# Gate and up projections in column blocks of 512, 512 and 384, with five shared PSUM banks and new orders on all engines

## What is computed

```python
v = x @ W_write.T                      # chunked decay recurrence over the sequence
reads = sum over earlier tokens j of decay**(t-1-j) * (x_t . x_j) * v_j
x = layernorm(2 * x + alpha * (reads @ W_read.T))
gate = fp4(x) @ fp4(w_gate).T          # w_gate, w_up: 704 x 256
up   = fp4(x) @ fp4(w_up).T
h    = silu(gate) * up                 # 704 columns
x = layernorm(x + fp4(h) @ fp4(w_down).T)
```

## Time and profile before

| | before |
|---|---|
| median of 3 runs | 328.34 us (328.29 to 328.41) |
| the profiled execution | 328.27 us, its span in the trace 326.5 us |
| PE busy | 317.1 us, 97% of the span, 2271 matmuls |
| weight loads (PEld) busy | 304.1 us, 93% |
| DVE busy | 291.2 us, 89% |
| POOL busy | 241.2 us, 74% |
| ACT busy | 211.8 us, 65% |
| TensorE clock granted | 0.996 of 2.4 GHz, mean |

### The profile page before, as it was taken

The page is one execution under the profiler, slowest core; times in us unless marked ns, Lnnn a source line. Parts: engine busy times, 40 slices in busy tenths (PEclk is TensorE's granted clock), DMA queues, the critical chain, the costliest instruction groups (busy, mean ns, idle before and its releaser), DMA issues.

```text
span 326.5 us, 6927 instructions
## 1 busy us (share of the span) xinstructions
PE 317.1 (97%) x2271; PEld 304.1 (93%) x2271; DVE 291.2 (89%) x754; ACT 211.8 (65%) x516; POOL 241.2 (74%) x257
## 2 busy tenths in 40 slices
PE   8899999999999999999999999999999999999993
PEld 3599999998999999999999999999999999999983
DVE  3999989989988889978898888998999999999972
ACT  3678975875485658466593658747684657665773
POOL 1589968977897777767797676967597767668772
PEclk9999999999999999999999999999999999999998
DMA  5804120030013000210003010002000001000011
GB/s 194 328 2 129 46 86 2 1 131 0 0 23 141 3 32 2 98 64 18 18 19 112 32 35 1 18 16 82 1 18 32 3 0 35 33 6 28 19 49 64
DMA packets 8243, 15.71 MB, mean 48 GB/s; under 512 B 1168, under 2 KB 5264, under 8 KB 8208
## 3 DMA queue, kind: packets, MB, share of 16 engines
q1 hardware_dynamic: 7920, 15.27, 13.7%
q10 hardware_dynamic: 288, 0.00, 0.0%
HBM read 11.08 MB, written 4.19 MB: 47 GB/s over the span
## 4 chain that ended last, share of the span: by engine, by line
PE 69%; DVE 14%; ACT 6%; issue 5%; POOL 3%; DMA 2%; ACTq 0%; DVEq 0%; POOLq 0%
PE gu L1683 9%; PE gu L1687 9%; PE gu L1684 9%; PE bank L1683 6%; PE bank L1684 6%; PE bank L1687 6%; PE bank L1693 5%; PE bank L1697 5%; PE bank L1696 5%; PE bank L1771 5%; DVE h_g L1068 2%; DVE h_y L1063 2%; DVE w_raw L1174 2%; DVE hqT_lo L1202 2%; DMA scal<-in_log_alpha_dram 2%
## 5 line engine op out<-in xcount | busy, mean ns | idle before, releaser
L1683 PE MATMUL gu<-guT_hi,xqT_hi 128*128 128x352 f32 x256 | 85.3, 334 | 0.2
L1684 PE MATMUL gu<-guT_lo,xqT_hi 128*128 128x352 f32 x256 | 82.2, 322 | 0.0
L406 POOL TENSOR_TENSOR h_q<-h_g,h_ns 128x704 f32<-128x704 f32 x32 | 49.2, 1537 | 38.9 <-DVE h_g L1068 36.7
L1687 PE MATMUL gu<-guT_hi,xqT_lo 128*128 128x352 f32 x256 | 61.7, 322 | 0.0
L399 POOL TENSOR_TENSOR h_n<-w_raw,h_rs 128x704 f32<-128x704 f32 x32 | 45.5, 1426 | 5.9 <-DVE h_rs L1058 5.6
L1683 PEld LDWEIGHTS gu<-guT_hi,xqT_hi 128*128 128x128 f32 x256 | 48.1, 188 | 0.9 <-DVE w_raw L1174 0.7
L1684 PEld LDWEIGHTS gu<-guT_lo,xqT_hi 128*128 128x128 f32 x256 | 48.2, 188 | 0.1
L1687 PEld LDWEIGHTS gu<-guT_hi,xqT_lo 128*128 128x128 f32 x256 | 44.5, 188 | 0.0
L694 ACT CAST hqT_hi<-bank 128x512 fp32r<-128x512 f32 x64 | 29.8, 475 | 15.2 <-PE bank L1771 13.6
L1684 PE MATMUL bank<-dnT_lo,hqT_hi 128*128 128x256 f32 x160 | 39.1, 279 | 0.0
L1683 PE MATMUL bank<-dnT_hi,hqT_hi 128*128 128x256 f32 x160 | 39.1, 279 | 0.0
(11 more groups left out here) (127 smaller groups left out, 888.3 us busy)
## 6 DMA issues: line engine op xcount, KB each, us to landing
x_full<-in_xt_rows_dram SPq DMA_DIRECT2D x8, 512.0 KB, 3.3
xs<-in_x_rows_dram SPq DMA_DIRECT2D x8, 512.0 KB, 3.4
out_dram<-wq_gu SPq DMA_DIRECT2D x32, 128.0 KB, 1.7
w_raw<-in_w_ffn_dram SPq DMA_DIRECT2D x6, 352.0 KB, 7.7
w_pair<-in_w_attn_dram SPq DMA_DIRECT2D x1, 512.0 KB, 7.2
scal<-in_decay_dram ACTq DMA_DIRECT2D x1, 0.5 KB, 3.1
scal<-in_log_alpha_dram ACTq DMA_DIRECT2D x1, 0.5 KB, 4.9
```

The lines of the kernel that those rows point to most:

```text
L406: nc.gpsimd.tensor_tensor(blocks(h_q[:, p, 0:I]), blocks(h_g[:, p, :]), per_block(h_ns[:, p, :], HB), ALU.mult).then_inc(h_quant, 1)
L1683: nc.tensor.matmul(dst, lh, rh, start=(first and i == 0), stop=False)
L1684: nc.tensor.matmul(dst, lh, rl, start=False, stop=False)
L1687: last = nc.tensor.matmul(dst, ll, rh, start=False, stop=(end and i == len(terms) - 1))
```

## The change

`LEFT` is 704 - 512 = 192. Gate and up of a tile now take three blocks: gate columns 0 to 511 in `gu[0]`, up columns 0 to 511 in `gu[1]` (both in the call with `half` 0), and in the call with `half` 1 the last 192 gate and 192 up columns side by side in `gu[2]`, as one block of 384. For this the host packs the weight rows in the order gate[:512], up[:512], gate[512:], up[512:]. A tile takes 12 matmuls of 512 and 6 of 384 columns. `gate_silu` and `hidden` work on 512 columns for half 0 and 192 for half 1. What they compute is the same.

The bank `gu[3]` is no longer needed by gate and up and joins the shared banks: `combine`, one of the `reads`, one of the `xq_transpose`, one `h_transpose` part and one `down` move to it, and others swap banks. The semaphores that the PE calls wait for follow these tables.

The lists of PE, ACT, DVE and POOL are put into a new order throughout; the number of steps on each is the same. On SP `store(0, 0)` moves ahead of `load_x_transposed(5)`, and `load_x(4)`, `load_x(5)` and `load_x(6)` each one step earlier. The diff, cut to its core (indentation shortened):

```diff
@@ constants and banks @@
+LEFT = I - 512
-v_bank, xq_bank = (bank[2], bank[1]), (bank[0], bank[2])
-s_bank, r_bank = (bank[1], bank[3], bank[0], bank[3]), (bank[2], bank[3])
-h_bank = ((bank[1], bank[0]), (bank[1], bank[0]), (bank[0], bank[2]), (bank[0], bank[2]))
-d_bank = (bank[3], bank[1], bank[3], bank[2])
-w_bank = (bank[0], gu[:, 3, :], bank[0], gu[:, 2, :], gu[:, 1, :], gu[:, 0, :], bank[0], bank[2], bank[2])
+v_bank, xq_bank = (bank[2], bank[1]), (gu[:, 3, :], bank[2])
+s_bank, r_bank = (bank[0], bank[3], bank[0], bank[3]), (gu[:, 3, :], bank[3])
+h_bank = ((bank[1], bank[0]), (bank[1], gu[:, 3, :]), (bank[0], bank[2]), (bank[0], bank[2]))
+d_bank = (bank[3], bank[1], bank[3], gu[:, 3, :])
+w_bank = (bank[1], gu[:, 3, :], bank[0], gu[:, 2, :], gu[:, 1, :], gu[:, 0, :], bank[2], bank[1], bank[2])
+part = (slice(0, 512), slice(512, I))
+gate_of, up_of = (gu[:, 0, :], gu[:, 2, 0:LEFT]), (gu[:, 1, :], gu[:, 2, LEFT:2 * LEFT])
@@ SP queue @@
     load_x(3)
+    store(0, 0)
     load_x_transposed(5)
-    store(0, 0)
+    load_x(4)
     store(1, 1)
-    load_x(4)
     store(2, 2)
     store(3, 3)
     store(4, 0)
     load_x_transposed(6)
+    load_x(5)
     store(5, 1)
-    load_x(5)
     store(6, 2)
     store(7, 3)
     store(8, 0)
     load_x_transposed(7)
+    load_x(6)
     store(9, 1)
-    load_x(6)
     store(10, 2)
@@ gate_silu (ACT) @@
-        nc.scalar.activation(silu[:, p, half * HALF:(half + 1) * HALF], gu[:, 2 * half, 0:HALF],
-                             ACT.Silu).then_inc(silu_ready, 1)
+        nc.scalar.activation(silu[:, p, part[half]], gate_of[half], ACT.Silu).then_inc(silu_ready, 1)
@@ hidden (DVE) @@
-        c = slice(half * HALF, (half + 1) * HALF)
+        c = part[half]
-        nc.vector.tensor_tensor(h[:, p, c], silu[:, p, c], gu[:, 2 * half + 1, 0:HALF],
-                                ALU.mult).then_inc(h_ready, 1)
+        nc.vector.tensor_tensor(h[:, p, c], silu[:, p, c], up_of[half], ALU.mult).then_inc(h_ready, 1)
@@ scale_comb (DVE) @@
-        nc.vector.tensor_scalar(comb[:], bank[3][:, 0:DK * D], scal[:, 3:4], None,
+        nc.vector.tensor_scalar(comb[:], gu[:, 3, :][:, 0:DK * D], scal[:, 3:4], None,
@@ first steps of DVE @@
     w_magic_add(0)
+    w_to_grid(0)
     x_rest(0, 0)
     x_rest(0, 1)
-    w_to_grid(0)
@@ gate_up (PE) @@
-        for m in range(2):
-            w = slice(m * I + half * HALF, m * I + (half + 1) * HALF)
-            last = split_matmuls(gu[:, 2 * half + m, 0:HALF],
+        for m in range(2 - half):
+            w = slice(1024, 2 * I) if half else slice(512 * m, 512 * m + 512)
+            last = split_matmuls(gu[:, 2, 0:2 * LEFT] if half else gu[:, m, :],
@@ first steps of PE @@
     combine([])
     scores(0, 0, [])
-    scores(0, 1, [(comb_ready, 1)])
-    scores(0, 2, [])
-    scores(0, 3, [(pr_ready, 2)])
+    scores(0, 1, [])
+    scores(0, 2, [(pr_ready, 1)])
     pe.wait_ge(comb_lo_ready, 1)
     values(0, 0, [])
-    values(0, 1, [(pr_ready, 1)])
-    reads(0, 0, [(v_lo_ready, 1)])
-    w_transpose(0, [(pr_ready, 3)])
+    scores(0, 3, [(pr_ready, 2)])
+    values(0, 1, [])
+    reads(0, 0, [(comb_ready, 1)])
     reads(0, 1, [(pr_ready, 4)])
+    w_transpose(0, [(v_lo_ready, 2)])
+    w_transpose(1, [(z_ready, 1)])
+    scores(1, 0, [(pr_ready, 3)])
     w_subtract(0)
-    scores(1, 0, [(v_lo_ready, 2)])
     scores(1, 1, [(z_ready, 2)])
...
@@ loop body of PE @@
-        gate_up(k - 1, b - 1, 3, 0)
+        h_transpose(k - 5, 3, 1, [(hT_lo_ready, 2 * k - 10)])
+        gate_up(k - 1, b - 1, 3, 1)
+        scores(n + 1, 0, [(hT_lo_ready, 8 * n - 17)])
+        gate_up(k, b, 0, 0)
         reads(n, 1, [(o_ready, 4 * n - 9)])
-        xq_transpose(n - 1, 0, [(hT_lo_ready, 8 * n - 17)])
-        gate_up(k - 1, b - 1, 3, 1)
-        h_transpose(k - 4, 0, 0, [(pr_ready, k + 9)])
+        values(n + 1, 0, [(hT_lo_ready, 8 * n - 16)])
+        h_transpose(k - 4, 0, 0, [(v_lo_ready, 2 * n + 2)])
+        down(k - 5, 3, [(xqT_lo_ready, 2 * n - 1)])
+        h_transpose(k - 4, 0, 1, [(pr_ready, k + 9)])
         scores(n + 1, 1, [(z_ready, 2 * n + 2)])
-        down(k - 5, 3, [(hT_lo_ready, 2 * k - 8)])
-        gate_up(k, b, 0, 0)
-        h_transpose(k - 4, 0, 1, [(xqT_lo_ready, 2 * n - 1)])
         gate_up(k, b, 0, 1)
         h_transpose(k - 3, 1, 0, [(hT_lo_ready, 2 * k - 7)])
-        values(n + 1, 0, [(o_ready, 4 * n - 8)])
-        gate_up(k + 1, b, 1, 0)
         scores(n + 1, 2, [(hT_lo_ready, 8 * n - 14)])
         down(k - 4, 0, [(pr_ready, k + 10)])
-        h_transpose(k - 3, 1, 1, [(pr_ready, k + 11)])
+        xq_transpose(n - 1, 1, [(v_lo_ready, 2 * n + 3)])
+        h_transpose(k - 3, 1, 1, [(o_ready, k - 4)])
+        gate_up(k + 1, b, 1, 0)
+        h_transpose(k - 2, 2, 0, [(pr_ready, k + 11)])
+        scores(n + 1, 3, [(o_ready, 4 * n - 7)])
         gate_up(k + 1, b, 1, 1)
-        reads(n + 1, 0, [(v_lo_ready, 2 * n + 3)])
+        reads(n + 1, 0, [(hT_lo_ready, 8 * n - 12)])
         down(k - 3, 1, [(hT_lo_ready, 2 * k - 5)])
-        xq_transpose(n - 1, 1, [(z_ready, 2 * n + 3)])
-        h_transpose(k - 2, 2, 0, [(hT_lo_ready, 2 * k - 4)])
-        scores(n + 1, 3, [(o_ready, 4 * n - 7)])
+        gate_up(k + 2, b, 2, 0)
+        gate_up(k + 2, b, 2, 1)
+        h_transpose(k - 2, 2, 1, [(xqT_lo_ready, 2 * n)])
+        h_transpose(k - 1, 3, 0, [(hT_lo_ready, 2 * k - 3)])
         values(n + 1, 1, [(o_ready, 4 * n - 6)])
-        gate_up(k + 2, b, 2, 0)
-        h_transpose(k - 2, 2, 1, [(xqT_lo_ready, 2 * n)])
-        gate_up(k + 2, b, 2, 1)
-        h_transpose(k - 1, 3, 0, [(hT_lo_ready, 2 * k - 3)])
-        h_transpose(k - 1, 3, 1, [(hT_lo_ready, 2 * k - 2)])
+        gate_up(k + 3, b, 3, 0)
+        xq_transpose(n, 0, [(z_ready, 2 * n + 3)])
         down(k - 2, 2, [(pr_ready, k + 12)])
-        scores(n + 2, 0, [(v_lo_ready, 2 * n + 4)])
     run(body)
...
@@ PE's order behind the loop, tiles 22 to 24, as it is after @@
+    gate_up(22, 5, 2, 1)
     h_transpose(19, 3, 0, [(hT_lo_ready, 37)])
     values(7, 1, [(o_ready, 18)])
     gate_up(23, 5, 3, 0)
+    scores(7, 3, [(o_ready, 17)])
+    gate_up(23, 5, 3, 1)
     h_transpose(19, 3, 1, [(hT_lo_ready, 38)])
+    gate_up(24, 6, 0, 0)
     down(18, 2, [(pr_ready, 32)])
     h_transpose(20, 0, 0, [(v_lo_ready, 16)])
+    gate_up(24, 6, 0, 1)
+    h_transpose(20, 0, 1, [(hT_lo_ready, 39)])
+    gate_up(25, 6, 1, 0)
...
@@ end of PE's order @@
     gate_up(28, 7, 0, 0)
     gate_up(28, 7, 0, 1)
-    h_transpose(24, 0, 1, [(xqT_lo_ready, 15)])
-    down(23, 3, [(hT_lo_ready, 48)])
+    h_transpose(24, 0, 0, [(o_ready, 22)])
+    h_transpose(24, 0, 1, [(hT_lo_ready, 47)])
+    gate_up(29, 7, 1, 0)
+    xq_transpose(7, 1, [(hT_lo_ready, 48)])
+    down(23, 3, [(xqT_lo_ready, 15)])
+    gate_up(29, 7, 1, 1)
     h_transpose(25, 1, 0, [(hT_lo_ready, 49)])
-    h_transpose(25, 1, 1, [(hT_lo_ready, 50)])
-    gate_up(29, 7, 1, 0)
-    xq_transpose(7, 1, [(o_ready, 24)])
-    gate_up(29, 7, 1, 1)
+    h_transpose(25, 1, 1, [(o_ready, 24)])
     down(24, 0, [(o_ready, 23)])
+    h_transpose(26, 2, 0, [(hT_lo_ready, 50)])
     gate_up(30, 7, 2, 0)
-    h_transpose(26, 2, 0, [(hT_lo_ready, 52)])
     gate_up(30, 7, 2, 1)
     h_transpose(26, 2, 1, [(xqT_lo_ready, 16)])
-    gate_up(31, 7, 3, 0)
     down(25, 1, [(hT_lo_ready, 51)])
     h_transpose(27, 3, 0, [(hT_lo_ready, 53)])
+    gate_up(31, 7, 3, 0)
     h_transpose(27, 3, 1, [(hT_lo_ready, 54)])
+    down(26, 2, [(o_ready, 25)])
+    h_transpose(28, 0, 0, [(o_ready, 26)])
+    h_transpose(28, 0, 1, [(hT_lo_ready, 55)])
     gate_up(31, 7, 3, 1)
-    h_transpose(28, 0, 0, [(o_ready, 26)])
-    down(26, 2, [(o_ready, 25)])
-    h_transpose(28, 0, 1, [(hT_lo_ready, 55)])
-    down(27, 3, [(hT_lo_ready, 56)])
+    down(27, 3, [(hT_lo_ready, 52)])
     h_transpose(29, 1, 0, [(hT_lo_ready, 57)])
-    h_transpose(29, 1, 1, [(hT_lo_ready, 58)])
     down(28, 0, [(o_ready, 27)])
-    h_transpose(30, 2, 0, [(hT_lo_ready, 60)])
-    h_transpose(30, 2, 1, [(o_ready, 28)])
+    h_transpose(29, 1, 1, [(o_ready, 28)])
+    h_transpose(30, 2, 0, [(hT_lo_ready, 58)])
+    h_transpose(30, 2, 1, [(hT_lo_ready, 56)])
     down(29, 1, [(hT_lo_ready, 59)])
+    down(30, 2, [(o_ready, 29)])
     h_transpose(31, 3, 0, [(hT_lo_ready, 61)])
     h_transpose(31, 3, 1, [(hT_lo_ready, 62)])
-    down(30, 2, [(o_ready, 29)])
-    down(31, 3, [(hT_lo_ready, 64)])
+    down(31, 3, [(hT_lo_ready, 60)])
@@ host packing @@
-"w_ffn": _np.concatenate([tiled(_np.concatenate([gate, up])), tiled(down)], axis=1),
+"w_ffn": _np.concatenate([tiled(_np.concatenate([gate[:512], up[:512], gate[512:], up[512:]])), tiled(down)], axis=1),
```

More of the change, by code:

```diff
@@ new lines, in body @@
+                x_to_grid(n, 0)
+                h_magic_add(k - 1, 1)
+                hidden(k + 1, 1, 0)
+                out_moments(k - 4, 0)
+                x_residual(n + 1, 0)
+                xq_rest(n - 1, 1)
+                h_rest(k - 2, 2, 0)
+                decay_scores(n + 1, 3)
```

(64 more changed lines are left out.)

1197 lines of the change are left out of this document (569 added, 628 removed).

## The result

The changed kernel takes 330.54 us (median of 15 runs, 329.12 to 331.8), the kernel before 328.41 us beside it (15 runs, 328.29 to 328.58): ratio 1.0058, interval 1.0049 to 1.0067. It is slower by 0.6%, where the prediction said 0.3% faster. The runs after lie in two groups, four at 329.1 to 329.2 and ten at 330.4 to 330.8 (one at 331.8); the profiled one, 330.54 us with a span of 328.8, is of the large group. Experiment 4 bears on the groups.

What follows compares the result with a forecast made beforehand. PE was taken as the bound, busy 97% of the span, with DVE also full from 231 us. Matmuls 0.9, start 0.3, end -0.1 made 1.1 us less than 328.27: 327.2 us, range 325.4 to 329.3.

Steps and rivals of the forecast that it cites:

- The start: Up to the first `reads`: the wait for `combine`'s bank goes, `reads` at 20.4 against 20.69 us; gain 0.3 us.
- Fewer, wider matmuls: Gate and up on PE: 18 matmuls a tile in place of 24, same columns; 0.9 us saved over 32 tiles.
- ACT and DVE: silu and `hidden` on 512 and 192 columns: `hidden` 1022 against 1006 ns a tile, half a us over the kernel.
- the 98% that the prediction drew as its line: Sign in the changed kernel's trace: DVE's share from 231 us at 98% or below.
- the rival in which DVE takes over: From 231 us DVE sets the pace, so PE's saving counts only elsewhere: 327.7 us, at most the old time; 22%.
- The order in the middle: New lists and shared banks between start and end: no change of waits, bounds 2 us less and 3 us more.
- "less than 2": Sign: the prediction is wrong if PE's waits between 26 and 305 us exceed 4 us or total under 2.
- "slower" rival: Single set of gate and up banks: late `hidden` at three places makes PE wait, 3.1 us; 329.3 us; 21%.
- The fourth case, banks that pay: Five shared banks remove most of the middle's 3 us of waits, 1.9 us more: 325.3 us; 15%.
- The end: Last gate and up to last matmul: later gate and up, better order behind the last transposes; 0.1 us given back.
- Sum: Whole kernel: 0.9 + 0.3 - 0.1 = 1.1 us less than the profiled 328.27, so 327.2 us.

Runs made afterwards that it cites:

- Experiment 4: Changed kernel with twelve bf16 matmuls on zeros on PE between the high and low part of `scores(0, 0)`: 329.11 us.
- experiment 5: Changed kernel with POOL's `w_dequant(0)` moved behind `p_rest(0, 0)`: 330.05 us.
- experiment 3: Kernel before, with its orders and banks, and only the new blocks of 512, 512 and 384 columns: 337.74 us.
- experiment 1: Changed kernel with `w_to_grid(0)` put back behind the two `x_rest` on DVE: 328.22 us.
- experiment 8: experiment 1 with both `x_rest` ahead of `w_magic_add(0)` on DVE as well: 329.05 us.

## Why the prediction was wrong, step by step

**The start** is the step that failed, from "Gain 0.3 us": the first `reads` came at 22.86 us where it said 20.4, which is 2.5 of the 3.3 us between forecast and result. Its walk along the lists was sound for what it counted: it put the low part at 14.05, the end of `scores(0, 0)` at 15.0 and `scores(0, 2)` at 16.15, and in experiment 5, without contention, these are 13.9, 14.93 and 16.05. It left out two things. It asked what the moved `w_to_grid(0)` delays, and not what it releases: `w_dequant(0)` on POOL, which stood in the trace right behind it, with 1.39 us. That held the low part back to 15.02 us, for 0.9 us at the end. And with the idle time on PE more than doubled, which it could have read from its own 14.05, it didn't ask for the clock: 1.4 us more. What the Trainium skill says in the section quoted in experiment 5 speaks against this very move, and was not weighed. The bound "between 0 and 0.5" was too narrow in consequence: it had no case for a delay.

**Fewer, wider matmuls:** 0.9 us was forecast, and it is nothing. Two rows of the timeline of the changed kernel give the columns' price:

```profile
158.33 0.40 PE L1685 MATMUL gu<-guT_lo,xqT_hi 128*128 128x512 f32 x1
...
160.90 0.60 PE L1772 MATMUL bank<-ident,h_q 128*128 128x128 f32 x4
```

Eleven starts in 2.57 us, 233.6 ns for 512 columns; over all tiles the medians are 233.8 for 512 and 175.3 for 384, so 12 x 233.8 + 6 x 175.3 = 3.857 us a tile against 3.859. The mechanism (as good as no fixed part in a matmul) was right, the size of the term wrong: the prediction took 231.5 ns from the slope between 256 and 352 columns although its own row for 512 gave 233. A 1.5 ns difference in 384 instructions is 0.6 us, two thirds of what was claimed. With 233 the term would have been 0.5 us, and a range for it would have reached to nothing.
All calls of `gate_up` together fell from 126.9 to 126.0 us, but not by a lower price: that is in the first and last start of a call, next to waits and transposes, and the other calls behind the first `reads` grew by as much, from 171.7 to 172.5 us.

**ACT and DVE:** `hidden` on 512 and on 192 columns takes 673 and 342 ns, 1015 a tile against 1006, as the steps said. DVE's share is:

```profile
231.00:270.00 39.00, 39.00 (x260) 35.89 (x260) 37.52 (x99) 24.91 (x64) 28.30 (x30) 1.00 0.05 15
```

96%, under the 98% that the prediction drew as its line: the rival in which DVE takes over did not happen.

**The order in the middle** held in its time: from first `reads` to last matmul it is the same within 0.1 us. Counted as what a call on PE takes beyond the fastest of its kind, the kernel before has five waits of over 0.25 us between the first `reads` and the last gate and up, 2.4 us in all (the longest two in the earlier trace rows), and the changed one four of 0.3 to 0.4 us, 1.5 us in all, ahead of `scores` or `down`. By the prediction's own line ("less than 2") that is a miss, and it brought nothing, since smaller gaps grew. Tiles 24 and 29 have no idle time ahead of `gate_up`, though only 1.7 to 1.9 us lay between:

```profile
251.16 0.38 PE L1772 MATMUL bank<-ident,h_q 128*128 128x128 f32 x2
251.30 0.48 PE L1684 MATMUL gu<-guT_hi,xqT_hi 128*128 128x512 f32 x1
...
286.55 0.82 PE L1772 MATMUL bank<-ident,h_q 128*128 128x128 f32 x6
287.12 0.48 PE L1684 MATMUL gu<-guT_hi,xqT_hi 128*128 128x512 f32 x1
```

So the "slower" rival came nearest to the time, with 329.3 for 330.54, by the wrong mechanism; that is luck. The mechanism exists: it is at least a part of what experiment 3 pays 9.4 us for. In the changed kernel it doesn't appear. The fourth case, banks that pay, fell too: fewer long waits did appear, and the end did not come nearer.

**The end** went nearly as walked. In the changed kernel:

```profile
309.42 0.51 PE L1688 MATMUL gu<-guT_hi,xqT_lo 128*128 128x384 f32 x2
309.77 0.28 PE L1782 MATMUL gu<-dnT_hi,hqT_hi 128*128 128x256 f32 x1
...
319.78 0.87 PE L1772 MATMUL bank<-ident,h_q 128*128 128x128 f32 x6
...
321.44 0.39 PE L1782 MATMUL gu<-dnT_hi,hqT_hi 128*128 128x256 f32 x1 [0.79 <-ACT hqT_hi L696]
```

Last gate and up to last transposes 10.01 us, 0.4 more than the 9.65 said; `down(31)` 1.66 us behind them, where 1.65 to 1.67 was said and 2.71 stood before. In experiment 1, with the start as it was, these are 307.49, 317.50 and 319.16 us, against 305.35, 316.58 and 319.29 before: the better order behind the transposes gives back what the later gate and up took, and 0.1 us is left. The last gate and up ends 2.1 us later than before there, where the walk had 2.7 us less the 0.9 saved; the 0.6 us by which it beats the 2.7 went for the greater part into the 0.4 us above. (Two parts of `h_transpose` went ahead with `down(26)`, not three; the 2.7 us fit the two.)

**Sum:** 327.2 + 2.5 (start) + 0.9 (columns) - 0.1 (given back and not needed) = 330.5.

## What to carry to other kernels

When a step is moved forward on one engine, look up what its semaphore releases and what runs there at that moment: `x_rest` on VectorE and the product on GpSimd, 1.28 and 1.39 us alone, took 2.47 us side by side, nearly the sum of their times. Price an idle time of PE near the start with the clock behind it, not only with its length. And where the saving is a difference of two large products (384 times 231.5 ns here), take the unit price from the row of that very shape; a 1% slip in it was the whole gain.

## What the runs showed of the hardware that was not expected

- `x_rest`, 512 columns times two: 1.28 us with POOL idle, 1.64 to 1.68 with the mask (0.61 us) beside it, 2.47 with the product on 704 columns beside it, which itself goes from 1.39 to 1.76. In experiment 8 the mask goes from 0.61 to 1.07 us and the pair to 1.85.
- TensorE's granted clock was 0.54 and 0.61 in the two stretches behind an idle time of 2.45 us in the changed kernel, which had been running at 1.00, and cost 1.4 us; in experiments 5 and 8, single idle times of 1.27 and 1.63 us at about the same place left it at 1.00 in the next stretches. In experiment 5 it fell to 0.50 later, behind two of 0.43 and 1.36 us. In experiment 5's six runs the mean clock parts two of 331.4 and 331.7 us (0.992, 0.991) from four of 329.9 to 330.1 (0.996 and more).
- float32 matmuls cost 0.457 ns a column at 352, 384 and 512 columns alike (160.8, 175.3 and 233.8 ns), 10% above one column per cycle of 2.4 GHz; what causes the 10% was not tried.
